# Cross attention's first keys, values and two contexts made inside self attention's last bodies

## What is computed

```python
x_norm = modulate(_ln(x), shift_a, scale_a)
q, k, v = jnp.split(x_norm @ W_qkv + b_qkv, 3, axis=-1)        # (16, 224, 512) each
attn_w = jax.nn.softmax(jnp.einsum('bhqd,bhkd->bhqk', q, k) * scale, axis=-1)
x = x + gate_a[:, None] * ((attn_w @ v as (B, N, H)) @ W_proj + b_proj)
q_c = _ln(x) @ W_qc + b_qc
k_c, v_c = jnp.split(_ln(context) @ W_kvc + b_kvc, 2, axis=-1)  # (16, 750, 512) each
x = x + cross_attention(q_c, k_c, v_c) @ W_cproj + b_cproj
x = x + gate_m[:, None] * (gelu(modulate(_ln(x), shift_m, scale_m) @ W_mlp1 + b_mlp1) @ W_mlp2 + b_mlp2)
```

## Time and profile before

| | |
|---|---|
| time, median of 3 runs | 2722.87 us (2719.10 to 2723.86) |
| the profiled execution | 2719.26 us, its span 2717.2 us |
| TensorE busy | 2620.2 us, 96% of the span |
| VectorE, ScalarE, GpSimd busy | 64%, 42%, 48% |
| TensorE's granted clock, mean | 0.98 of full speed |
| steady self bodies | 43 us each, from 88 to 691 us |
| self attention's last matmul, barrier left | 766.1 us, 773.8 us |
| first cross scores, first transposed ones | 817.6 us, 838.8 us |

### The profile page before, as it was taken

How to read it: one execution, slowest core, us unless ns; L and a number is a source line. 1 busy time by engine, 2 the same in 40 slices (tenths; PEclk the granted TensorE clock), 3 DMA queues, 4 the chain that set the end, 5 groups by cost and what they waited for, 6 DMA issues and landing times. The chain is left out here.

```text
span 2717.2 us, 50012 instructions
## 1 busy us (share of the span) xinstructions
PE 2620.2 (96%) x18612; PEld 2152.4 (79%) x18612; DVE 1732.6 (64%) x3477; ACT 1130.3 (42%) x2187; POOL 1295.9 (48%) x1447
## 2 busy tenths in 40 slices
PE   8999999999879999999999999999799999999997
PEld 6688888888677888888888888887478888888886
DVE  6777777777737777777777777766654444444431
ACT  4344444444434555555555555554432212212210
POOL 1444445353524777777777777777611220220211
PEclk9999999999889999999999999999799999999999
DMA  8454444545343444444444444434331111111110
GB/s 226 129 130 117 127 122 123 136 115 126 115 127 97 112 113 110 113 116 116 113 109 116 119 113 113 108 96 116 91 113 36 43 47 36 43 47 36 43 43 24
DMA packets 170769, 269.86 MB, mean 99 GB/s; under 512 B 30849, under 2 KB 84609, under 8 KB 170513
## 3 DMA queue, kind: packets, MB, share of 16 engines
q1 hardware_dynamic: 167456, 259.33, 34.8%
q0 software_dynamic: 3072, 7.34, 0.8%
HBM read 111.11 MB, written 36.77 MB: 54 GB/s over the span
## 5 line engine op out<-in xcount | busy, mean ns | idle before, releaser
L1643 ACT ACTIVATE cross_prT<-cross_tr_ps 125x448 f32<-125x448 f32 x768 | 407.0, 544 | 284.1 <-PE cross_tr_ps L1393 275.2
L1521 DVE TENSOR_REDUCE cross_parts<-cross_sc_ps 112x1 f32<-112x500 f32 x512 | 336.6, 663 | 211.9 <-PE cross_sc_ps L1379 210.8
L1694 POOL TENSOR_TENSOR cross_part<-cross_prT 125x448 f32<-125x448 f32 x252 | 291.2, 1156 | 211.7 <-PE cross_or_ps L1413 111.8
L1017 POOL TENSOR_TENSOR self_psum<-self_prT 112x224 f32<-112x224 f32 x256 | 173.8, 679 | 349.6 <-ACT self_prT L907 340.0
L1393 PE MATMUL cross_tr_ps<-cross_qst,cross_kst 98*125 98x224 f32 x1536 | 312.4, 287 | 4.9 <-ACT cross_prT L1643 3.3
L1393 PEld LDWEIGHTS cross_tr_ps<-cross_qst,cross_kst 98*125 98x125 f32 x1536 | 256.6, 189 | 62.2 <-ACT cross_prT L1643 23.5
L1696 POOL TENSOR_TENSOR cross_part<-cross_part,cross_prT 125x448 f32<-125x448 f32 x252 | 291.8, 1158 | 19.7
L2091 ACT ACTIVATE mlp_hv<-mlp_h_ps,mlp_b 128x512 f32<-128x512 f32 x112 | 76.9, 687 | 519.8 <-PE mlp_h_ps L73 505.8
L1379 PE MATMUL cross_sc_ps<-cross_kst,cross_qst 96*112 96x500 f32 (+1 forms) x1024 | 262.2, 337 | 3.0 <-DVE cross_parts L1521 2.6
L2008 DVE CAST mlp_hT_h<-mlp_hv 128x512 fp32r<-128x512 f32 x112 | 52.2, 466 | 320.6 <-ACT mlp_hv L2091 320.6
L907 ACT ACTIVATE self_prT<-self_st_ps 112x448 f32<-112x448 f32 x256 | 138.8, 543 | 210.0 <-PE self_st_ps L487 209.9
(11 more groups left out here) (275 smaller groups left out, 6768.8 us busy)
## 6 DMA issues: line engine op xcount, KB each, us to landing
cross_kst<-cross_nat_h SPq DMA_DIRECT2D x512, 93.8 KB, 2.2
cross_c_in<-in_context SPq DMA_DIRECT2D x96, 250.0 KB
cross_kst<-cross_nat_l SPq DMA_DIRECT2D x256, 93.8 KB, 2.2
cross_qst<-qc SPq DMA_DIRECT2D x192, 112.0 KB, 2.4
self_kst<-self_nat_h SPq DMA_DIRECT2D x128, 112.0 KB, 2.3
self_qst<-self_natq_h SPq DMA_DIRECT2D x128, 112.0 KB, 2.9
self_x_in<-in_x SPq DMA_DIRECT2D x16, 448.0 KB, 3.6
self_kst<-self_nat_l SPq DMA_DIRECT2D x64, 112.0 KB, 2.3
```

What stands on the lines that cost most here:

```text
L1017: pool.tensor_tensor(psum[:, j], prT[:, j, 0], prT[:, j, 1], ALU.add).then_inc(p_summed, 1)
L1521: dve.tensor_reduce(parts[:, g % 2, j, u, 0:1], sc_ps[u][0:QN, 0:SHALF[0]], AX_X, ALU.max, negate=True).then_inc(maxed, 1)
L1643: act.activation(prT[:, slot(h), 2 * c:2 * c + 2], bank(h, c)[0:SN, 0:2 * N].rearrange("p (k t) -> p k t", k=2), ACT.Exp).then_inc(exped, 1)
L1694: pool.tensor_tensor(part[:], prT[:, j, 0:2], prT[:, j, 2:4], ALU.add).then_inc(pre_summed, 1)
```

## The change

Cross attention's first work moves into self attention's bodies 15 and 16. The loads of `w_kvc` and of context 0 are issued in body 14, ahead of `place_maxima(b, 2)`; context 1 is loaded in body 15 from ScalarE's queue. VectorE takes context 0's statistics in steps 0 to 2 of body 15, ScalarE normalises it in steps 5 and 6, TensorE transposes its six tiles in steps 6 to 8 (`turn_context`) and makes value tiles 0 and 1 in steps 9 and 10 (`cross_v`). Body 16 gets value tiles 2 to 5 in steps 0 to 3, the eight key halves in steps 6 to 9 (`cross_k`), ahead of `pv`, and context 1's tiles in steps 10 and 11. Their evictions go to ScalarE (`high_context`, `keep_v`, `high_k`) and VectorE (`low_context`, `low_k`). The semaphores that both phases need live in a class `Seam`, and buffers are laid out anew (`Room`), so that the made tensors survive the barrier. Cross attention then starts by stacking keys, part of it from ScalarE's queue (`first_stack`), and scores at once.

In all bodies the maxima are transposed unsplit, one transpose for four heads and both tiles, and split on VectorE after it; two DMAs put them in place. `qst` is laid out by group, then head. "ty" pieces sit one step later in `FILL`, and VectorE evicts the first piece of a step before its row maximum, and normalises last.

```diff
-        FILL = [[("c", 1, 1), ("k", 0, 0)], [("k", 0, 1)], [("k", 1, 0)], [("k", 1, 1), ("ty", 0, 0)],
-                [("q", 0, 0), ("ty", 1, 0)], [("q", 0, 1), ("q", 1, 0)], [("q", 1, 1)], [("v", 0, 0)],
+        FILL = [[("c", 1, 1), ("k", 0, 0)], [("k", 0, 1)], [("k", 1, 0)], [("k", 1, 1)],
+                [("q", 0, 0), ("ty", 0, 0)], [("q", 0, 1), ("q", 1, 0), ("ty", 1, 0)], [("q", 1, 1)], [("v", 0, 0)],
...
+        TILES_AT, NEXT_TILES_AT = {6: (0, 1), 7: (2, 3), 8: (4, 5)}, {10: (0, 1, 2), 11: (3, 4, 5)}
+        V_AT, LATE_V_AT, K_AT = {9: 0, 10: 1}, {0: 2, 1: 3, 2: 4, 3: 5}, {6: (0, 1), 7: (2, 3), 8: (4, 5), 9: (6, 7)}
...
+        def v_bank_free(t):
+
+            return (seam.cT_l, 5 + t) if t < 2 else (maxed, B * NH) if t < 4 else (seam.v_done, t - 1)
...
             def place_maxima(b, g):
                 sp.wait_ge(m_row, b.n(KC, g + 1))
-                sp.dma_start(qst[TERMS * HD:ROWS, b.par, :, g].bitcast(F32), mrow[:].bitcast(F32)).then_inc(m_in, 16)
+                for s in range(2):
+                    sp.dma_start(qst[TERMS * HD + s:TERMS * HD + s + 1, b.par, g].bitcast(F32), mrow[s][:].bitcast(F32)).then_inc(m_in, 16)
...
                 if nxt:
                     stack(a, q_l, natq, qst, q_stacked, (0, 0, 1))
+                if b.c == B - 2:
+                    sp.wait_ge(v_ps, 2 * B)
+                    load_context()
+                    load_wkv()
                 if att:
                     place_maxima(b, 2)
-                if b.c == B - 2:
-                    load_wkv()
...
+                if part == 0 and kind == "p" and o.c == B - 2:
+                    pe.wait_ge(seam.v_done, c + 1)
...
+                    if b.c == B - 1 and h in V_AT:
+                        cross_v(V_AT[h])
+                    if b.c == B and h in LATE_V_AT:
+                        cross_v(LATE_V_AT[h])
+                    for i in K_AT.get(h, ()) if b.c == B else ():
+                        cross_k(i)
...
             def split_maxima(b, g):
-                dve.wait_ge(maxed, b.n(NH, HPG * (g + 1)))
-                wait(dve, m_ps, b.n(KC, g - 1))
-                dve.tensor_copy(nsplit[:, g % 2, :, 0], nmax[:, g % 2]).then_inc(m_h, 1)
+                turned = tx_ps[0:HPG * QT, 0:QN]
+                dve.wait_ge(m_ps, b.n(KC, g + 1))
+                wait(dve, m_in, b.n(32 * KC, 32 * g))
+                dve.tensor_copy(mrow[0][:], turned).then_inc(m_h, 1)
                 dve.wait_ge(m_h, b.n(KC, g + 1))
-                dve.tensor_tensor(nsplit[:, g % 2, :, 1], nmax[:, g % 2], nsplit[:, g % 2, :, 0].bitcast(F32), ALU.subtract).then_inc(m_l, 1)
+                dve.tensor_tensor(mrow[1][:], turned, mrow[0][:].bitcast(F32), ALU.subtract).then_inc(m_row, 1)
...
-            sp.dma_start(bkv[:], b_kvc_t).then_inc(columns_in, 16)
-            load_q(Batch(0), 0)
-            for t in range(ST):
-                load_c(Batch(1), t)
-            load_q(Batch(0), 1)
-            for g in range(KC):
+            for g in range(2):
+                load_q(Batch(0), g)
+                first_stack(sp, g, 0)
+            for g in range(2, KC):
                 stack_k(Batch(0), g)
-                if g + 2 < KC:
-                    load_q(Batch(0), g + 2)
+                load_q(Batch(0), g)
             for t in range(ST):
                 load_c(Batch(2), t)
...
+            for g in range(2):
+                first_stack(act, g, 1)
+                first_stack(act, g, 2)
             bodies(act, body)
```

More of the change, by code:

```diff
@@ L102, in alloc, with __init__, take @@
     return sb, ps, sem
+class Room:
+    def __init__(self, nc, phase, at, end):
+        self.nc, self.phase, self.at, self.end = nc, phase, at, end
+    def take(self, name, shape, dt=F32):
+        words = 1
+        for n in shape[1:]:
+            words *= n
+        at, self.at = self.at, self.at + (4 * words + 31) // 32 * 32
+        assert self.at <= self.end
+        return self.nc.alloc_sbuf_tensor_at(f"{self.phase}_{name}", list(shape), dt, offset=at)
+class Seam:
+    def __init__(self, sem, bkv):
+        self.bkv, self.bkv_in = bkv, sem("bkv_in")
+        self.cT_ps, self.cT_h, self.cT_l = sem("cT_ps"), sem("cT_h"), sem("cT_l")
+        self.k_ps, self.k_h, self.k_l = sem("k_ps"), sem("k_h"), sem("k_l")
+        self.v_ps, self.v_done = sem("v_ps"), sem("v_done")
+SBUF_END = 224 * 1024
+KHALVES = ((0, 376), (376, S - 376))
 def self_phase(nc, x, cond_t, w_mod, b_mod, w_qkv, b_qkv_t, w_proj, b_proj, w_qc, b_qc_t, gates, x1, qc, mod_t,
-               context, w_kvc, wqkv, wqkv_raw, wkv, wkv_raw, c_in, ident, neg_half, eps):
+               context, w_kvc, b_kvc_t, wqkv, wqkv_raw, wkv, wkv_raw, c_in, seam, ident, neg_half, eps):
     with ExitStack() as ctx:
@@ L193, in self_phase @@
         wkv_h, wkv_l = sem("wkv_h"), sem("wkv_l")
-        c_loaded = [sem(f"c_loaded{t}") for t in range(ST)]
+        c_loaded = [sem(f"c_loaded{half}") for half in range(2)]
         stats_c, mvs_c, vareps_c, rstd_c, nmr_c, chat_c = (sem(s) for s in ("stats_c", "mvs_c", "vareps_c", "rstd_c", "nmr_c", "chat_c"))
@@ L1144, in cross_phase @@
         ORDER = [f for step in FILL for f in step]
-        FIRST = [("k", g, half) for g in range(KC) for half in range(2)] + [("v", t) for t in range(ST)]
-        FIRST_BANKS = (even_ps, odd_ps, sc_ps[0])
-        FIRST_TILES = {10: (0,), 11: (1, 2), 12: (3,), 13: (4, 5)}
         LAG = 6
@@ L1711, in _ @@
             pool.wait_ge(constant, 2)
-            for half in range(2):
-                inverse_std(Batch(1), half)
             bodies(pool, body)
@@ L1740, in mlp_phase @@
[L1740 to L1750 removed]
+        rows = lambda v: v.rearrange("(a n) -> a n", a=1).broadcast_to([P, H])
+        low = Room(nc, "mlp", low_at, seam.x_at)
@@ new lines, in mlp_phase @@
+        w2 = [low.take("w2_h", [P, MC, H], F32R)]
+        o_in = low.take("o_in", [P, KC, P])
+        middle = Room(nc, "mlp", seam.x_at + 4 * MLP, seam.kst_at)
+        at = middle.at
+        w2_raw = middle.take("w2_raw", [P, MC, H])
+        w2.append(nc.alloc_sbuf_tensor_at("mlp_w2_l", [P, MC, H], F32R, offset=at))
+        x2 = middle.take("x2", [P, 2 * GT, H])
+        xv = middle.take("xv", [P, KC, GN])
+        bcp = middle.take("bcp", [P, H])
+        bv, b1 = middle.take("bv", [P, KC]), middle.take("b1", [P, MC])
@@ new lines, in mlp_phase @@
+        turn = middle.take("turn", [1, 1])
+        st, mv = middle.take("st", [P, GT, 6]), middle.take("mv", [P, GT, 2])
+        ve, rs, nm = middle.take("ve", [P, GT]), middle.take("rs", [P, GT]), middle.take("nm", [P, GT])
+        xT = [Room(nc, "mlp", seam.kst_at + 4 * MLP, seam.nat_at[0]).take("xT_h", [P, KC, GN], F32R)]
+        high = Room(nc, "mlp", seam.nat_at[0] + 4 * MLP, seam.nat_at[1])
+        xT.append(high.take("xT_l", [P, KC, GN], F32R))
+        hT = [high.take(f"hT_{s}", [P, GR, GN], F32R) for s in "hl"]
@@ L1752, in mlp_phase @@
+        top = Room(nc, "mlp", seam.nat_at[1] + 4 * MLP, SBUF_END)
+        gate = top.take("gate", [P, 2, H])
+        oT = [top.take(f"oT_{s}", [P, KC, P], F32R) for s in "hl"]
+        x_in, b2, hv = top.take("x_in", [P, H]), top.take("b2", [P, H]), top.take("hv", [P, GN])
         h_ps = [ps(f"h_ps{i}") for i in range(2)]
```

373 lines of the change are left out of this document (215 added, 158 removed).

## The result

The changed kernel takes 2752.3 us (median of 4 runs, 2749.4 to 2754.4) against 2723.4 us of the kernel before on the same chip: a ratio of 1.0106, 95% interval 1.0091 to 1.0121. It is slower, as forecast, but by 29 us and not by 20; 2752.3 lies 1.3 us above the end of the range. The profiled run has a span of 2749.8 us, 32.6 more than before.

The account below looks back on a forecast made before the run. TensorE was taken to be full in steady bodies, with gaps in bodies 15 and 16. The terms summed as 2719.3 - 8 + 8.5 + 16.5 + 24 - 20.5 = 2739.8, forecast 2740 us, range 2720 to 2751.

Parts of the forecast that it names:

- Steady bodies: Self attention's steady bodies: one transpose fewer per group, 3.8 us, and fewer TensorE waits, about 6 us; -8 us (-10 to +3).
- Body 14: Third group's maxima land late behind context and weights, TensorE stands about 7 us at `score_t`, clock falls; +8.5 us (0 to +11).
- Body 15: VectorE's added statistics and low parts delay the first value tile, then two value tiles follow; +16.5 us (+9 to +19).
- body 16: Value tiles, key halves, context tiles and waits precede the last projection tile, 33.7 us less gaps; +24 us (+18 to +27).
- Cross attention's start: After the barrier, scores start early but VectorE waits for batch 2's load, TensorE behind it; -20.5 us (-37 to -17).
- The load is there in time: Rival: batch 2's first statistics don't wait, start gains 37 in place of 20.5 us: 2723, no change; chance 0.13.
- The gaps take the products: Rival: idle time and slow clock in bodies 15 and 16 absorb products, 20 us in place of 40.5: 2712; chance 0.12.
- The steady bodies lose: Rival: VectorE's evictions wait for ScalarE or the second DMA is late, +2 to +3 for -8: 2751; chance 0.1.

Follow-up runs that it names:

- the control with six tiles: Changed kernel with the first context loaded by six DMAs of one 125-partition tile each in place of two of three tiles; 2751.5 us in one run.
- the two runs: Changed kernel with 3 of 12 matmuls kept in each of batch 0's key halves, 2746.3 us, or in each of its value tiles, 2740.3 us.

## Why the prediction was right or wrong

**Steady bodies, -8, measured -9.8.** Right by two errors that cancel, so by luck. (The two gains that I named, 3.8 and 6, make 9.8; 8 was set down without a reason.) The steady gain is 1.2 us a body, twice what I put down. The earlier trace rows named 0.45 us of waits a body, and undoing the two orders cost 1.34; what else they save beside the named waits no run took apart. Against it, body 0 is longer: the first exponential of body 1 comes 4.4 us later than before. In body 0 the maxima stand behind the stacks in SyncE's queue, TensorE waits 3.7 us for `mrow_l`, and with VectorE's order back part of that loss goes. I had no term for the first body. The turn itself, -3.8 in my sum, gave nothing.

**Body 14, +8.5, measured +22.9.** This is the step that failed. Its mechanism was right: a small DMA behind two loads, TensorE at `score_t` behind it, a slow clock after (0.71 us for a matmul pair at 689.99, 0.37 in the earlier trace rows). The size was not: 20.2 us of waiting, not 7. "At that rate 3.6 MB take 9.5 us", with the rate of 381 GB/s, took the rate of the weights, which have 128 partitions, for the context, which has 125. The cut by partitions, the control with six tiles and the DMA views show that this load runs at 127 GB/s on a third of the engines. The right row was in the trace that I had: cross attention loads the same six tiles of 125 partitions there. The windows view of the kernel before, 825 to 832 us:

```profile
825.00:832.00 7.00, 5.53 (x31) 4.58 (x29) 5.76 (x13) 1.15 (x2) 0.00 (x0) 1.00 0.32 123
```

At 123 GB/s the context's 1.54 MB alone are 12.5 us, and a third of the engines has its third of the weights (0.7 MB) to carry as well, 5.7 us more: 18 us in place of 9.5, and a sum of about 2748.

The other 5 us or so are not the time of issuing. SyncE did stand 6.9 us in the weights' issues where the earlier trace rows has 1.82, but it had issued the maxima by 676.0, and in the DMA view a third of the engines or more is busy without a gap until 690. What the view and the packets show is that the context, alone from 668 to 672 at its 63 packets a microsecond, moved at 34 from 673 on, with the weights on all engines: it was through at 682 or so, some 4 us later than at its own rate. My sum had nothing for what two loads cost each other; how much of the 5 us is this no run took apart.

**Body 15, +16.5, measured +12.9, and body 16, +24, measured +26.8.** Together 39.7 for 40.5. The first value tile came 26.2 us after the reciprocal (forecast 28.6 or later; the terms given there make 28.9), so body 15's error is that VectorE took less than my prices. That the products are paid in the main, the values nearly in full and the keys at half or less, is shown by the two runs; the bound in the prediction that these bodies grow by 30 us or more held. Self attention's last matmul is at 819.5 and not near 807: the 12 us are body 14's.

**Cross attention's start, -20.5, measured -20.6.** VectorE waited 14.2 us for the load (forecast over 12), until 33.0 us after the barrier and not 30.6: SyncE needed 28.4 us for its 44 DMAs, not 26.2. So 20.6 us were won there and not 22.9. (The 38 us that the text gives for a start without the wait don't come out of its own terms, 53.5 less 7.4 and 5 to 6: that is 40 to 41.) The 2.5 us that I took off for half clock after the wait don't show (-0.5 to the end), so two errors of 2.4 us cancel, which is luck again.

**The rivals.** *The load is there in time* came true in two runs. With the load moved forward in the queue it brought nothing; with the load out of the queue it brought 12 to 14 us, not 16.5, for there VectorE came to the first statistics 18.3 us after the barrier, not the 13 that my text has. *The gaps take the products* fell: the two bodies grew by 39.7 us and not by 20. *The steady bodies lose* gave a time near the measured one for a wrong reason, since they won. The missing 12 us are in none of them: a rival that priced the context's load apart from the weights' would have held them.

## What to carry to other kernels

Price a transfer by a row of the same shape, partitions first, not by the best rate that the trace has; a load of 125 partitions ran on a third of the engines here, and what stands behind such a load in the queue waits as well. Another queue is no cure by itself: the engines are shared, and the engine that issues may be the one that is needed. Where a small transfer is needed every few microseconds, long loads belong between two of them, each short enough for the gap, and not ahead of one in a block; that order and the cut by partitions together were worth 22 us here (2740.1 to 2718.1). A queue that is full after a barrier isn't mended by its order: take out what can be loaded before.

## What the runs showed of the hardware

- A load of 125 partitions kept the DMA share at 0.32 to 0.33 and some 123 to 127 GB/s (the kernel before, the changed one and the control), in DMAs of three tiles or of one; cut into 112 and 13 partitions the share was 1.00 and context and weights together moved at 300 GB/s.
- Issuing is not a fixed price. The same four weight loads took 1.82 us to issue on SyncE, 6.86 behind the context, 13.54 on ScalarE behind the context, and 2.7 on ScalarE behind the context cut by partitions. An engine that computes should not be the one that issues behind a slow load.
- A small DMA ahead of a load in the queue is still slowed by it: 15.5 us of waiting in place of the 11 that were estimated for the context alone; the load ahead fell from 63 to 34 packets a microsecond.
- A small DMA in another queue than the loads can wait as well: 9.9 us, with all 16 engines busy.
